# Mixer: u's transposes in three banks and one B/C tile inside the y products; attention: group 0's pieces spread, seam pieces reordered

## What is computed

```python
def mixer(x, ...):                       # 8 heads of 64, 16 states per head
    zgate, u, Bc, Cc, dt = split(x @ in_proj_w.T)
    u, Bc, Cc = silu(conv4(u, Bc, Cc))   # causal, 4 taps
    Bc, Cc = Bc * rsqrt(sum(Bc**2)), Cc * rsqrt(sum(Cc**2))
    dt = softplus(dt + dt_bias)
    def step(z, y):                      # over the 112 tokens
        z = (z + d * (u * B - A * y)) / (1 + d * d * A)
        y = y + d * z
        out = einsum(y, C)
    return ((ys + D_skip * u) * silu(zgate)) @ out_proj_w.T + out_proj_b

x = layernorm(x + block(x))              # block: mixer, then gelu MLP 256-1024-256
q, (k, v) = xn @ Wq, cn @ Wkv            # 16 heads of 64 queries, one k and v
out = softmax(q @ k.T / 8 + mask) @ v @ Wout + (silu(gate) * value) @ W2
x = layernorm(x + out)
x = layernorm(x + quantize(quantize(relu(x @ w1.T + b1)) @ quantize(w2.T)))
```

## Time and profile before

| what | us |
|---|---|
| median of 3 runs | 1895.42 (1892.58 to 1896.31) |
| the profiled execution's own time | 1893.93 |
| its span in the trace | 1892.1 |
| PE busy | 1783.0 (94%) |
| DVE busy | 1302.0 (69%) |
| ACT busy | 927.1 (49%) |
| POOL busy | 420.1 (22%) |
| mean granted PE clock | 0.981 of full |

### The profile page before, as it was taken

The page is one execution under the profiler, slowest core; times in us unless marked ns, Lnnn a source line. Parts: engine busy times, 40 slices in busy tenths (PEclk is TensorE's granted clock), DMA queues, the critical chain, the costliest instruction groups (busy, mean ns, idle before and its releaser), DMA issues.

```text
span 1892.1 us, 27875 instructions
## 1 busy us (share of the span) xinstructions
PE 1783.0 (94%) x9320; PEld 1035.3 (55%) x9320; DVE 1302.0 (69%) x3970; ACT 927.1 (49%) x2262; POOL 420.1 (22%) x569
## 2 busy tenths in 40 slices
PE   4579999999999999999999999999999999999997
PEld 2346666666667544455445554545545545555466
DVE  6888988988957587476567557657737656755743
ACT  3353563463441456446445545545645644554542
POOL 4866876876861010000000000000000000000000
PEclk8789999999999999999999999999999999999999
DMA  4000001001014242232222222222222222222200
GB/s 129 11 10 21 11 21 30 11 21 31 1 38 148 59 152 73 51 75 73 63 64 67 72 70 58 59 66 79 58 63 76 74 59 63 70 60 70 54 13 20
DMA packets 75181, 106.13 MB, mean 56 GB/s; under 512 B 11456, under 2 KB 68736, under 8 KB 74144
## 3 DMA queue, kind: packets, MB, share of 16 engines
q1 hardware_dynamic: 74576, 103.90, 20.2%
q10 hardware_dynamic: 464, 0.46, 0.1%
HBM read 96.92 MB, written 7.42 MB: 55 GB/s over the span
## 4 chain that ended last, share of the span: by engine, by line
PE 76%; DVE 17%; DMA 2%; issue 2%; ACT 1%; POOL 1%; SPq 0%; DVEq 0%; POOLq 0%; ACTq 0%
PE ps L1500 20%; PE ps L1455 9%; PE ps L1462 9%; PE ps L1493 9%; PE ps L1478 8%; DVE m_u L725 3%; PE ps L404 3%; PE ps L388 3%; PE ps L314 2%; DVE m_rs L757 2%; PE ps L1560 2%; PE ps L439 2%; PE ps L1600 1%; PE ps L1554 1%; PE ps L424 1%
## 5 line engine op out<-in xcount | busy, mean ns | idle before, releaser
L1839 DVE CUSTOM_DVE_ANT_0 x_pr<-ps,x_mk 128x375 f32<-128x375 f32 x448 | 227.6, 545 | 312.1 <-issue 200.0
L1711 ACT ACTIVATE x_pT<-ps 125x384 f32<-125x384 f32 x448 | 195.4, 489 | 269.2 <-PE ps L1462 268.2
L1717 ACT ACTIVATE x_pr<-x_pr,x_mx 128x375 f32<-128x375 f32 x448 | 268.2, 608 | 34.5 <-DVE x_mx L1839 34.4
L1462 PEld LDWEIGHTS ps<-ident,x_pr 128*125 128x125 f32 x1344 | 163.6, 187 | 129.2 <-issue 91.2
L1455 PE MATMUL ps<-x_kT,x_qT 64*128 64x375 f32 x896 | 204.0, 530 | 23.7 <-DVE x_mx L1839 17.7
L1462 PE MATMUL ps<-ident,x_pr 128*125 128x128 f32 x1344 | 206.0, 290 | 0.0
L1500 PE MATMUL ps<-x_xn,x_w 128*128 128x448 f32 x512 | 203.8, 541 | 0.0
L1848 DVE TENSOR_SCALAR x_pr<-x_pr,x_rc 128x375 f32<-128x375 f32 x448 | 169.4, 421 | 8.0
L1478 PE MATMUL ps<-x_pT,x_va 125*64 125x512 f32 (+1 forms) x768 | 160.2, 553 | 0.6 <-ACT x_pT L1711 0.6
L314 PE MATMUL ps<-m_xa,w_in 128*128 128x448 f32 x352 | 145.1, 563 | 6.2 <-ACT m_xa L530 6.2
L1455 PEld LDWEIGHTS ps<-x_kT,x_qT 64*128 64x128 f32 x896 | 68.7, 186 | 144.0 <-issue 115.4
(11 more groups left out here) (196 smaller groups left out, 2880.8 us busy)
## 6 DMA issues: line engine op xcount, KB each, us to landing
x_mk<-in_mask SPq DMA_DIRECT2D x224, 187.5 KB, 2.4
x_cx<-in_context SPq DMA_DIRECT2D x32, 375.0 KB
x_cT<-in_context_turned SPq DMA_DIRECT2D x32, 375.0 KB, 3.2
x_rb<-context_roots SPq DMA_DIRECT2D x32, 187.5 KB, 5.1
m_Rd<-bc_roots SPq DMA_DIRECT2D x8, 448.0 KB, 3.4
x_mixed<-m_x SPq DMA_DIRECT2D x8, 448.0 KB, 3.7
X<-x_mixed SPq DMA_DIRECT2D x8, 448.0 KB, 3.8
m_X<-in_x SPq DMA_DIRECT2D x7, 448.0 KB, 4.0
```

What stands on the lines that cost most here:

```text
L1462: last = pe.transpose(bank(2 + e)[0:JP, t * ROWS:(t + 1) * ROWS], pr[:, 2 * (p % SLOT) + e, t * JP:(t + 1) * JP], ident[:, :])
L1711: act.activation(pT[:, 2 * NV * (batch(p) % 2) + 2 * (p % NP % NV) + e, :, :].rearrange("p t s -> p (t s)"), bank(2 + e)[0:JP, 0:JT * ROWS ...
L1717: act.activation(pr[:, k, :], pr[:, k, :], ACT.Exp, scale=-1.0, bias=mx[:, k:k + 1], accum_out=sums[:, k:k + 1]).then_inc(h_e.sem, 1)
L1839: dve.tensor_tensor_reduce(pr[:, k + e, :], bank(e)[:, 0:J], mk[:, p % SLOT, :], -1.0, 3.0e38, ALU.add, ALU.min, mx[:, k + e:k + e + 1]).t ...
```

## The change

In the mixer: the turned u goes through banks 0, 1 and 2 in place of 0 and 1, and the MLP's first layer takes bank 3 first and bank 2 second in place of 2 and 3. The next group's tile 1 (B) is multiplied between y product 2 and y product 3. On DVE, sequence 0's `causal_part` of the next scan stands between the reciprocal and the two `m_E` products of `factors`. In the last group the second layer's results go to banks 4 and 5 in place of twice bank 4.

In attention: the turn of step 26 stands ahead of `scores(0)` of the next group in place of behind it; the output product's first two quarters stand in steps 0 and 1 (before: 1 and 2); the final norm's stages stand in steps 26, 27, 27 (before: 25, 26, 27). In group 0 the 16 gate and value tiles are spread over steps 10 to 23 (before: two in each of 10 to 17), the next tokens' norm is in steps 16, 17 and 20 (before: 20, 21, 22), the four `down_token` pieces are in steps 0 to 3 (before: 1 to 4), the weight conversion is in step 5 (before: 8), `MLP_NORM` in 12 (before: 11; two of SP's transfers follow it), and one root, one norm and the first stage of one context's norm are done before group 0 begins.

```diff
-        def bc_tiles(i):
+        def bc_tile(i, n):
             hold(pe, b_mc, i - 1, 6)
-            for n in (1, 2):
-                in_tile(n, bank(n - 1)[:, 0:T])
+            in_tile(n, bank(n - 1)[:, 0:T])
...
             for b in range(GB):
-                if b >= 2:
-                    hold(pe, a_uTc, i, b - 1)
+                if b == 3:
+                    pe.wait_ge(a_uTc.sem, a_uTc.value(i, 1))
...
                 if b >= 1:
                     scan_out(b - 1)
+            if i + 1 < NG:
+                bc_tile(i + 1, 1)
             scan_out(GB - 1)
...
             for n in range(KH):
+                if n == 1 and i + 1 < NG:
+                    pe.wait_ge(a_uTc.sem, a_uTc.value(i + 1, 3))
...
-                    last = pe.matmul(bank((2, 3, 6)[n % 3])[:, 0:T], ...
+                    last = pe.matmul(bank((3, 2, 6)[n % 3])[:, 0:T], ...
...
-        def factors(i):
+        def factors(i, between=None):
...
             dve.reciprocal(Rs[:, :], Rs[:, :]).then_inc(a_dt.sem, 1)
+            if between is not None:
+                causal_part(between, 0)
...
-            causal_part(i, 0)
+            if i == 0 or i == LAST:
+                causal_part(i, 0)
...
-                factors(i + 2)
+                factors(i + 2, between=i + 1)
...
-RESULT, TOKENS, FINAL = (10, 11, 12), (20, 21, 22), (25, 26, 27)
+RESULT, TOKENS, TOKENS_FIRST, FINAL = (10, 11, 12), (20, 21, 22), (16, 17, 20), {STEPS - 2: (0,), STEPS - 1: (1, 2)}
...
-            at[4 * c + n + 1, "Y"].append(("out", c, n))
+            at[4 * c + n + (1 if c or n >= 2 else 0), "Y"].append(("out", c, n))
...
+def schedule_first(at):
+    first = {place: [piece for piece in at[place] if piece[0] not in ("gate", "value")] for place in at}
+    tiles = [(kind, f) for f in range(KH) for kind in ("gate", "value")]
+    for n, piece in enumerate(tiles):
+        first[W1_AT + n * 7 // 8, "Y"].append(piece)
+    return first
...
-MLP_DOWN, MLP_SUM, MLP_ROOT, MLP_NORM = (1, 2, 3, 4), (2, 4), 10, 11
+MLP_DOWN, MLP_SUM, MLP_ROOT, MLP_NORM = (0, 1, 2, 3), (2, 4), 10, 12
...
             for p in range(STEPS):
+                if p == 0 and not first:
+                    turn(*back(it, p, 2))
                 scores(it, p)
...
-                if p >= 2 or not first:
+                if p >= 2 or (p == 1 and not first):
                     turn(*back(it, p, 2))
...
-                if first and p == 0:
-                    roots_result(LAST - 1, 2)
-                if first and p == 1:
-                    normed_result(LAST - 1)
...
-                if first and p == 8:
+                if first and p == 5:
...
         context_norm(-1, 0, 2)
+        roots_result(LAST - 1, 2)
+        normed_result(LAST - 1)
         part(-1, ("kv", 0))
+        context_norm(0, 1, 0)
         part(-1, ("vback", 0))
```

More of the change, by code:

```diff
@@ L355, in turn_u @@
             for b in range(GB):
-                if b >= 2:
-                    hold(pe, a_uTc, i, b - 1)
+                if b == 3:
+                    pe.wait_ge(a_uTc.sem, a_uTc.value(i, 1))
                 for k in range(KI):
-                    last = pe.transpose(bank(b % 2)[0:S, k * 128:(k + 1) * 128], ua[:, k, b * S:(b + 1) * S], ident[:, :])
+                    last = pe.transpose(bank(b % 3)[0:S, k * 128:(k + 1) * 128], ua[:, k, b * S:(b + 1) * S], ident[:, :])
                 last.then_inc(a_uT.sem, 1)
@@ L423, in hidden @@
                 for k in range(KD):
-                    last = pe.matmul(bank((2, 3, 6)[n % 3])[:, 0:T], fc1[:, k, n * 128:(n + 1) * 128], xb[:, k, :],
+                    last = pe.matmul(bank((3, 2, 6)[n % 3])[:, 0:T], fc1[:, k, n * 128:(n + 1) * 128], xb[:, k, :],
                                      start=(k == 0), stop=(k == KD - 1))
@@ L435, in down @@
             for b in range(b0, b1):
-                if i == LAST and b == 2:
-                    pe.wait_ge(b_s.sem, b_s.value(LAST, 1))
                 for k in range(KH):
-                    last = pe.matmul(bank(4 + b // 2 if i < LAST else 4)[0:S, (b % 2) * D:(b % 2 + 1) * D], gl[:, k, b * S:(b + 1) * S], fc2[:, k, :],
+                    last = pe.matmul(bank(4 + b // 2)[0:S, (b % 2) * D:(b % 2 + 1) * D], gl[:, k, b * S:(b + 1) * S], fc2[:, k, :],
                                      start=(k == 0), stop=(k == KH - 1))
@@ L451, in tensor @@
         dt_tile(0)
-        bc_tiles(0)
+        bc_tile(0, 1)
+        bc_tile(0, 2)
         pe.wait_ge(s_wb.sem, 16)
@@ L461, in tensor @@
             if i + 1 < NG:
-                bc_tiles(i + 1)
+                bc_tile(i + 1, 2)
             out_project(i, i + 1 < NG)
@@ L585, in turned_u @@
                 act.wait_ge(a_uT.sem, a_uT.value(i, b + 1))
-                act.activation(uT[:, b, :], bank(b % 2)[0:S, :], ACT.Copy).then_inc(a_uTc.sem, 1)
+                act.activation(uT[:, b, :], bank(b % 3)[0:S, :], ACT.Copy).then_inc(a_uTc.sem, 1)
         def heads(i, part):
@@ L607, in hidden @@
                 act.wait_ge(b_f1.sem, b_f1.value(i, n + 1))
-                act.activation(gl[:, n, :], bank((2, 3, 6)[n % 3])[:, 0:T], ACT.Gelu_apprx_tanh, bias=fb1[:, n:n + 1]).then_inc(b_gl.sem, 1)
+                act.activation(gl[:, n, :], bank((3, 2, 6)[n % 3])[:, 0:T], ACT.Gelu_apprx_tanh, bias=fb1[:, n:n + 1]).then_inc(b_gl.sem, 1)
         def tiles(i):
@@ L919, in result_half @@
             dst = x1[:, LAST % XR, 2 * c:2 * c + 2, :]
-            dve.tensor_tensor(dst, bank(4)[0:S, :].rearrange("p (b d) -> p b d", d=D), dst, ALU.add).then_inc(b_s.sem, 1)
+            dve.tensor_tensor(dst, bank(4 + c)[0:S, :].rearrange("p (b d) -> p b d", d=D), dst, ALU.add).then_inc(b_s.sem, 1)
             dve.wait_ge(b_s.sem, b_s.value(LAST, c + 1))
@@ L1081, in schedule @@
     return at
+def schedule_first(at):
[4 more added lines that the diff above has]
+    return first
 W1_AT = 10
 AT = schedule()
+AT_FIRST = schedule_first(AT)
 START = [("token", 0), ("token", 1), ("mlp", 0), ("mlp", 1), ("query", 0), ("mlp", 2), ("query", 1), ("mlp", 3), ("query", 2),
@@ L1110, in __init__ @@
     def __init__(self):
-        whole = [x for p in range(STEPS) for s in "XY" for x in AT[p, s]]
-        body = [x for x in whole if x[0] != "out" or x[2] == 3]
+        body, opening = ([x for p in range(STEPS) for s in "XY" for x in at[p, s] if x[0] != "out" or x[2] == 3] for at in (AT, AT_FIRST))
         self.start, _ = self.places(AHEAD)
-        self.first, n0 = self.places([("start",) + x for x in AHEAD] + [x for x in body if x not in BEHIND])
+        self.first, n0 = self.places([("start",) + x for x in AHEAD] + [x for x in opening if x not in BEHIND])
         self.body, self.per = self.places(body)
@@ L1580, in group @@
                 if first and p in MLP_DOWN:
+                    if p == MLP_DOWN[2]:
+                        emptied(pe, -1, ("vback", 0))
                     down_token(MLP_DOWN.index(p))
@@ L1664, in parts @@
                 pe.wait_ge(l_w1.sem, 16)
-            for piece in AT[p, slot]:
+            for piece in (AT_FIRST if first else AT)[p, slot]:
                 if not (first and piece in BEHIND) and not (last and piece in AHEAD):
@@ L1968, in group @@
                 b, r = divmod(p, NP)
-                if r in CONTEXT and not (last and b == GB - 1):
+                if r in CONTEXT and not (last and b == GB - 1) and not (first and p == 0):
                     context_norm(it, (b + 1) % GB, CONTEXT.index(r))
-                if p in TOKENS and not last:
-                    tokens_norm(it, TOKENS.index(p))
-                if first and p == 0:
-                    roots_result(LAST - 1, 2)
-                if first and p == 1:
-                    normed_result(LAST - 1)
+                at = TOKENS_FIRST if first else TOKENS
+                if p in at and not last:
+                    tokens_norm(it, at.index(p))
                 if first and p in MLP_SUM:
@@ L1993, in group @@
                     result_norm(it - 1, RESULT.index(p))
-                if not first and p in FINAL:
-                    final_norm(it - 1, FINAL.index(p))
+                for stage in FINAL.get(p, ()) if not first else ():
+                    final_norm(it - 1, stage)
         dve.sem_inc(f_s.sem, f_s.first)
```

## The result

| what | before | changed |
|---|---|---|
| median, us | 1895.87 (1892.58 to 1898.55, 4 runs) | 1872.18 (1871.41 to 1873.19, 4 runs) |
| the profiled execution's own time | 1893.93 | 1873.19 |
| its span | 1892.1 | 1871.4 |
| mean granted PE clock | 0.981 | 0.978 |

The ratio of the times is 0.9876, with a 95% interval of 0.9859 to 0.9893: 23.5 us faster, where 30.5 were forecast. 1872.18 us lies inside the range of 1859 to 1875.

A forecast was written before the change was run, and what follows sets the result against it. PE was taken to bound the kernel, with 34.9 us of its own waits. Savings of 8.7 (mixer) + 7.0 + 6.9 + 7.9 = 30.5 us took 1893.93 to 1863.4, forecast as 1865 us against the median; range 1859 to 1875.

The forecast's parts named there:

- What bounds the kernel: Whole kernel: PE, busy 94% of the span, has 34.9 us of waits, nearly all touched by the change.
- Mixer, y product 3: In seven scans the next group's tile 1 fills PE's 0.44 us wait for matrix 3's copy; 3.1 us saved.
- Mixer, the loop: Mixer's loop through DVE: copies ahead of `m_E` and a third bank bring y product 0 earlier; 5.3 us in five scans.
- Rival 1: The mixer's loop doesn't shorten, as y product 3's delay passes through DVE; 5 to 8.7 us lost; chance 0.12.
- Seams: Between attention groups, the earlier turn and output quarter remove waits after queries and for the first `highest`; 7.0 us saved.
- step 27: Attention groups 1 to 6: its scores stop waiting once the final norm's statistics stand behind `highest(26)`; 6.9 us saved.
- Group 0: Attention's first group: of 12.3 us from idle time and low clock, 4.4 us stay; 7.9 us saved.
- Rival 2: In attention's first group idle time only moves, as DVE's steps set the pace; 7.9 us lost, 1873 us; chance 0.13.
- Rival 4: PE's clock falls in group 0's steps 4 to 9 and stays low; 1905 us if half is slow; chance 0.03.

The follow-up runs named there:

- tile_behind: The changed kernel with the next group's B tile put back behind y product 3: 1873.32 us, ratio 0.9887 to the kernel before.
- after_late: The changed kernel with the halving of w2 on ACT in eight pieces and SP's loads of w2, wo, fw1 two steps later: 1864.19 us, ratio 0.9842.

## Why the prediction was right, and which term was not

- **What bounds the kernel: right.** PE's own waits, 34.9 us of them. The waits that were listed went, and the time fell by most of them.
- **Mixer, y product 3: right.** 3.1 us forecast for seven scans, 2.6 for the six that the periods hold; `tile_behind` gives 2.5.
- **Mixer, the loop: right, by 4.9 of 5.3 us.** The two edits came out at 2.9 and 2.0. "The smaller of 1.08 (DVE) and 0.5 + its present wait (PE)" is borne out only in part: by it nothing of the loop's gain is left without the moved copies, and 2.0 us are. Periods of 67.8 us against the 67.5 forecast: PE waits 0.19 to 0.29 us for the copies in five of the changed kernel's middle groups still, and up to 0.20 for the last silu. Rival 1 falls.
- **Seams and step 27: right, 14.8 us for 13.9.** Step 27 alone 7.0 for 6.9, the seams 7.8 for 7.0.
- **Group 0: wrong in size, 1.5 us for 7.9.** (Its leftovers add up to 4.3 or, with 0.4 us in each of steps 5 and 26, 4.7 us, not 4.4; that changes little.) Its working for steps 0 to 10 held: idle of 0.36, 1.06, 1.30 and 0.16 us in steps 5, 6, 9 and 10, 2.9 us in all where 0.4 + 1.5 + 1.4 = 3.3 were forecast, and no slow row in steps 1 to 10. What failed is the sentence that "SP's store of the last result and its weight loads come one or two steps later than before; a dozen steps lie between them and group 1, so nothing waits": a term put at nothing. The loads release POOL's halving, which held up a pair of DVE's divides by 3.6 to 5.1 us wherever it came, and the roots' store waits behind them. Both costs were hidden before: the 4.43 us row stood in DVE's timeline of before with no wait of PE beside it, since two tiles and a product with v lay over it, and the store's 6.8 us ended in time. One step later the halving met a step without that product and with the tokens' root in it, and the store stood right behind the loads. The two cost 4.3 and 1.9 us.
- **Rival 2 was near in time for another reason.** It gives 1873 us by group 0's idle moving, because DVE's steps set the pace. The time was 1872.18, but the cause was not this: with POOL and the queue out of the way the same steps run in 113.87 us.
- **Rival 4, the clock in steps 4 to 9: did not come.** Idles of up to 1.30 us there leave the scores at 0.90 us in every step, as the row-based count had it. Its limit of 1.6 us is no safe one, though: see the last section. The rule of the Trainium skill that stood for it ("TensorE: Matmul & The Clock Gate", on a second HAM failure mode) is not borne out in this stretch.

The forecast of 1865 us for the whole would have held but for this: `after_late`, the same change with the two uncovered costs taken away, took 1864.19. Part of that is luck, since the mixer's 1.4 us too few and the seams' 0.9 us too many nearly cancel. And 1872.18 us lies in the range because that had room for rivals 1 and 2, not because the range foresaw this cause.

## What to carry to other kernels

When work is thinned out over a stretch, list what the dense part was covering there: not the waits (a covered cost has none), but every row of the other engines that is longer than its like, and by how much it ends in time (here 0.46 us). A divide of 4.43 us among 0.74 us ones is such a row. Ask also what each moved DMA releases and which small transfer stands behind it in the queue. And compare stages over several profiles before a microsecond or two in one of them is explained.
